# Node roots on VectorE, node rows normalised behind the coming visit's rows, three row buffers

## What is computed

```python
x = x + segment_sum(layernorm(x)[src] * edge_weight[:, None], dst) @ W.T + b
h = layernorm(x)                      # (h - mean) / sqrt(var + 1e-5)
logits = h @ gate_w + gate_b
idx = argmax(softmax(logits)); prb = softmax(logits)[idx]
# a token keeps its place if fewer than C tokens before it chose its expert
y = relu(h @ w1[idx] + b1[idx]) @ w2[idx] + b2[idx]
x = x + y * prb * kept
```

## Time and profile before

| what | value |
|---|---|
| median of 3 runs | 2467.34 us (2462.58 to 2469.74) |
| the profiled execution | 2467.59 us, span 2465.7 us, mean granted TensorE clock 0.855 |
| PE busy | 1823.3 us (74%) |
| POOL busy | 1794.0 us (73%) |
| DVE busy | 1164.4 us (47%) |
| ACT busy | 1099.5 us (45%) |

### The profile page before, as it was taken

How to read it: one execution, slowest core, us unless ns; L and a number is a source line. 1 busy time by engine, 2 the same in 40 slices (tenths; PEclk the granted TensorE clock), 3 DMA queues, 4 the chain that set the end, 5 groups by cost and what they waited for, 6 DMA issues and landing times.

```text
span 2465.7 us, 35440 instructions
## 1 busy us (share of the span) xinstructions
PE 1823.3 (74%) x9798; PEld 1185.8 (48%) x9798; DVE 1164.4 (47%) x5806; ACT 1099.5 (45%) x2565; POOL 1794.0 (73%) x1873
## 2 busy tenths in 40 slices
PE   2333466666888898777777777776887887787699
PEld 1111233333555565455444544554554555554698
DVE  7767443334454454444444444344544544444332
ACT  5667523333545454344434434343543444453343
POOL 6677777777777677777777777777777777777571
PEclk9999975555988899788888888888988988998799
DMA  6566433335553564445445454544554455556567
GB/s 225 187 210 200 121 105 113 113 112 190 155 156 114 161 214 117 152 118 188 118 116 190 116 188 118 188 117 154 155 190 154 117 191 155 190 156 189 180 237 266
DMA packets 139883, 397.04 MB, mean 161 GB/s; under 512 B 36197, under 2 KB 62821, under 8 KB 129046
## 3 DMA queue, kind: packets, MB, share of 16 engines
q0 software_dynamic: 89712, 244.29, 33.4%
q1 hardware_dynamic: 46276, 137.66, 16.2%
q10 hardware_dynamic: 3698, 12.80, 1.4%
HBM read 498.88 MB, written 42.89 MB: 220 GB/s over the span
## 4 chain that ended last, share of the span: by engine, by line
POOL 52%; issue 19%; PE 13%; DVE 8%; ACT 5%; DMA 1%; SPq 0%; DVEq 0%; POOLq 0%; ACTq 0%
POOL msg L621 49%; PE ps L980 5%; ACT msg L735 3%; POOL rows_by_expert L649 3%; DVE wsl L1136 3%; PE ps L968 2%; PE ps L879 2%; PE ps L870 1%; PE ps L959 1%; DVE wsl L1139 1%; DMA hin<-rows_by_expert 1%; DMA msg<-normed,src_sb 1%; POOL out_x L655 1%; ACT wsl L701 0%; PE ps L950 0%
## 5 line engine op out<-in xcount | busy, mean ns | idle before, releaser
L621 POOL DMA_INDIRECT msg<-normed,src_sb x1462 | 1398.1, 956 | 457.4 <-issue 445.2
L870 PE MATMUL ps<-msg,onehot 128*32 128x256 f32 x3332 | 435.2, 505 | 231.1 <-DMA msg<-normed,src_sb 206.9
L1177 DVE TENSOR_TENSOR aggT<-aggT,ps 128x192 f32 x294 | 104.7, 356 | 879.8 <-PE ps L879 856.1
L980 PE MATMUL ps<-wsl,hmid 128*128 128x256 f32 x1680 | 401.4, 394 | 1.5 <-ACT hmid L791 1.5
L744 ACT COPY pairs<-ps 128x256 f32<-128x256 f32 x294 | 111.4, 379 | 618.5 <-PE ps L870 617.6
L879 PE MATMUL ps<-shift,pairs 128*128 128x96 f32 x1176 | 237.3, 334 | 180.5 <-ACT pairs L744 180.5
L980 PEld LDWEIGHTS ps<-wsl,hmid 128*128 128x128 f32 x1680 | 322.9, 197 | 71.9 <-issue 29.5
L950 PE MATMUL ps<-wsl,hTf 128*128 128x512 f32 x680 | 350.1, 662 | 0.5 <-ACT hTf L777 0.5
L870 PEld LDWEIGHTS ps<-msg,onehot 128*32 128x32 f32 x3332 | 139.7, 128 | 413.1 <-DMA msg<-normed,src_sb 256.8
L879 PEld LDWEIGHTS ps<-shift,pairs 128*128 128x128 f32 x1176 | 191.6, 231 | 246.0 <-ACT pairs L744 242.1
L791 ACT ACTIVATE hmid<-ps,wsl 128x128 f32<-128x128 f32 x840 | 230.5, 381 | 133.3 <-PE ps L968 71.2
(11 more groups left out here) (128 smaller groups left out, 2283.3 us busy)
## 6 DMA issues: line engine op xcount, KB each, us to landing
wsl<-in_wsecond SPq DMA_DIRECT2D x105, 1152.0 KB
wsl<-in_wfirst SPq DMA_DIRECT2D x105, 1028.0 KB
msg<-normed,src_sb POOLq DMA_INDIRECT x1462
xrow<-in_x SPq DMA_DIRECT2D x97, 128.0 KB, 2.3
wsl<-in_x SPq DMA_DIRECT2D x24, 512.0 KB, 4.1
normed<-wsl ACTq DMA_DIRECT2D x24, 512.0 KB, 3.0
hin<-rows_by_expert SPq DMA_DIRECT2D x89, 130.0 KB
msg<-in_x,src_sb POOLq DMA_INDIRECT x204
```

The source lines that it names most:

```text
L621: pool.indirect_dma_start(out=msg[:, m + j, :], out_offset=None, in_=x if t < RAW else ln_dram, in_offset=bass.IndirectOffsetOnAxis(ap=src ...
L870: last = nc.tensor.matmul(ps[h * QWIN:(h + 1) * QWIN, t % 2, 0:D], onehot[:, j, :], msg[:, j, :], start=i == 0, stop=i == QUARTERS[q][h] - 1)
L980: last = nc.tensor.matmul(ps[:, Y, 0:D], hmid[:, c, :], w2_at(v % 2)[:, c, :], start=c == 0, stop=c == FC - 1)
```

## The change

The root of a node's variance is no longer ACT's. DVE computes the reciprocal root itself, in eight linked instructions: half of the variance plus epsilon; a first value from its bits, made with a negative sign; and three Newton steps of two instructions, each of which turns the sign, so that the third gives the positive result. The waits between DVE and ACT for it go. ACT's normalising of the node's tile becomes an event of its own, `nn`, which stands behind the load and the norm of the coming visit's rows and ahead of `turn`; at the end of the list it keeps its place behind `x2`. The rows of visits have three buffers instead of two, and two small tiles (`ids`, `fin`) now lie over the first 105 columns of the sources and the weights.

```diff
@@ schedule_of
         if coming is not None:
             once("hl", coming)
             once("hn", coming)
+        if stage[1] is not None:
+            events.append(("nn", stage[1]))
         events.append(("turn", t))
         events.append(("add", t))
...
-    events += [("gnn", a), ("ra", c), ("rk", c), ("x2", a), ("rb", c), ("pads",)]
+    events += [("gnn", a), ("ra", c), ("rk", c), ("x2", a), ("nn", a), ("rb", c), ("pads",)]
...
-    events += [("lg", a), ("ra", a), ("x2", b)]
+    events += [("lg", a), ("ra", a), ("x2", b), ("nn", b)]
@@ tiles and waits
+HBUFS = 3
+ROOT_BITS = float(0x5F3759DF - (1 << 22) - (1 << 31))
-        hin = sb("hin", [P, 2, ROW])
+        hin = sb("hin", [P, HBUFS, ROW])
-        ids = sb("ids", [P, V], I32)
-        fin = sb("fin", [P, V])
+        ids, fin = src_sb[:, 0:V], wgt[:, 0:V]
...
-                elif v >= 2:
-                    sp.wait_ge(s_z, v - 1)
+                elif v >= HBUFS:
+                    sp.wait_ge(s_z, v + 1 - HBUFS)
@@ scalar
-            def node_root(n):
-                act.wait_ge(s_mv, n + 1)
-                root(sd[:, :], mv[:, 1:2]).then_inc(s_sd, 1)
...
-                elif kind == "x2":
-                    node_root(key[0])
+                elif kind == "nn":
                     node_norm(key[0])
@@ vector, node(n)
-                dve.bn_aggr(mv[:, :], st6[:, :]).then_inc(s_mv, 1)
+                link(dve.bn_aggr(mv[:, :], st6[:, :]))
                 link.mark(dve.tensor_scalar(row[:, X_ID:X_ID + 1], pid, float(n * P), None, ALU.add))
-                dve.wait_ge(s_sd, n + 1)
-                link(dve.reciprocal(row[:, X_RSTD:X_RSTD + 1], sd[:, :]))
+                half, near, step = sd[:, 0:1], sd[:, 1:2], sd[:, 2:3]
+                link(dve.tensor_scalar(half, mv[:, 1:2], EPS, 0.5, ALU.add, ALU.mult))
+                link(dve.tensor_scalar(near.bitcast(I32), half.bitcast(I32), -0.5, ROOT_BITS, ALU.mult, ALU.add))
+                for to in (near, near, row[:, X_RSTD:X_RSTD + 1]):
+                    link(dve.scalar_tensor_tensor(out=step, in0=near, scalar=half, in1=near, op0=ALU.mult,
+                                                  op1=ALU.mult))
+                    link(dve.scalar_tensor_tensor(out=to, in0=step, scalar=-1.5, in1=near, op0=ALU.add,
+                                                  op1=ALU.mult))
```

More of the change, by code:

```diff
@@ L264, in gnn_moe_kernel @@
     assert max(V - NT, 0) * D + (V - FULL) * ROW <= RING * SUBS[0] * D
-    assert D == 2 * P and E8 == 8 and LAST_ROWS > 0 and NC * KD >= NT * D and V - NT <= G
+    assert V <= RAW_GROUPS * G and D == 2 * P and E8 == 8 and LAST_ROWS > 0 and NC * KD >= NT * D and V - NT <= G
     ln_dram = nc.dram_tensor("normed", (N, D), F32).ap()
@@ L287, in gnn_moe_kernel @@
         eps = sb("eps", [P, 1])
-        sd = sb("sd", [P, 1])
+        sd = sb("sd", [P, 3])
         wg_sb = sb("wg_sb", [P, KD, D])
@@ L358, in rows_at @@
             if v < FULL:
-                return hin[:, v % 2, :]
+                return hin[:, v % HBUFS, :]
             start = max(V - NT, 0) * D + (v - FULL) * ROW
@@ L363, in rows_sem @@
         def rows_sem(v):
-            return s_hin[v % 2] if v < FULL else s_last[v - FULL]
+            return s_hin[v % HBUFS] if v < FULL else s_last[v - FULL]
         def rows_used(v):
-            return 16 * (v // 2 + 1) if v < FULL else 16
+            return 16 * (v // HBUFS + 1) if v < FULL else 16
         space = wsl[:, :, :].rearrange("p a b -> p (a b)")
@@ L403, in gnn_moe_kernel @@
         s_xt = [sem(f"s_xt{u}") for u in range(XBUFS)]
-        s_n1, s_x2, s_mv, s_sd, s_stat, s_h, s_tr, s_hTs, s_log, s_ls, s_exp, s_choice, s_rank, s_route = (
-            sem(q) for q in ("s_n1", "s_x2", "s_mv", "s_sd", "s_stat", "s_h", "s_tr", "s_hTs", "s_log", "s_ls", "s_exp", "s_choice",
+        s_n1, s_x2, s_stat, s_h, s_tr, s_hTs, s_log, s_ls, s_exp, s_choice, s_rank, s_route = (
+            sem(q) for q in ("s_n1", "s_x2", "s_stat", "s_h", "s_tr", "s_hTs", "s_log", "s_ls", "s_exp", "s_choice",
                              "s_rank", "s_route"))
@@ L409, in gnn_moe_kernel @@
         s_plan = sem("s_plan")
-        s_hin = [sem(f"s_hin{b}") for b in range(2)]
+        s_hin = [sem(f"s_hin{b}") for b in range(HBUFS)]
         s_last = [sem(f"s_last{b}") for b in range(V - FULL)]
```

## The result

The changed kernel takes 2470.2 us, the kernel before 2465.1 us (medians of 15 runs each): a ratio of 1.0024, 95% interval 1.0014 to 1.0034. That is 5.1 us slower, inside the 0.3% that was called no change, where a gain to 2456.5 us was forecast, and 2 us above the stated range of 2450 to 2468 us. The profiled execution has a span of 2467.7 us against 2465.7.

What follows compares the result with a forecast made beforehand. POOL's gather issue was taken to bound the kernel, leaving only its 10.9 us wait between 600 and 900 us to gain, plus 0.2 us at the end: 2467.6 - 10.9 - 0.2 = 2456.5 us, range 2450 to 2468.

Steps and rivals of the forecast that it cites:

- What bounds the kernel: Whole loop: POOL's gather issue sets the pace; only its 10.9 us wait for PE, 600 to 900 us, can be gained.
- Roots off ACT: ACT: 98 roots and 194 table loads go, 278 us of busy time; worth nothing in the loop after 900 us.
- Eight DVE instructions: DVE's node chain: 2.12 us from moments to L1233 against 0.74, so the node comes 1.38 us later where ACT was ready.
- the norm's move: Dense stretch: copies and transposes up to 3.2 us earlier, second layer 2.0 us earlier, cycle 15.9 us instead of 17.9.
- the bound that I had named as enough: Dense stretch: any gain over 0.8 us a visit is enough to clear all 10.9 us of POOL's wait.
- a second layer at the lower clock as a rival: Dense-stretch cycle gains under 0.8 us: second layer 4.27 us instead of 3.46, 5 us come back, 2462.4 us; chance 0.08.
- the slower rival: POOL's gathers slowed by DVE's new operands, 26 us in all, so 2482.6 us; chance 0.07.
- Three buffers: Visits' row transfers: start up to 4.8 us earlier with a third buffer, costed at nothing since POOL's pace hides it.
- The end: After the last gather: node 96's DVE chain takes 2.1 us instead of 2.3, 0.2 us gained; the rest as before.
- The rival that the end gives it back: End: two short row landings become long, 9.3 us lost, so 2465.8 us, no change; chance 0.16.

Runs made afterwards that it cites:

- e1: The changed kernel with the root back on ScalarE and one reciprocal on VectorE, moved norm and three row buffers kept: 0.9967 of the kernel before, 2458.4 us.
- e12: The kernel before with only the node's norm moved behind the coming visit's rows, roots on ScalarE, two row buffers: 0.9973 of the kernel before, 2454.2 us.
- e5: The changed kernel with four unused products ahead of PE's wait for the slots, node tiles 15 to 33: 0.9967 of the kernel before, 2454.6 us.
- e11: The changed kernel with two row buffers instead of three, run where the kernel before takes 2461.2 us: 1.0027 of the kernel before.
- e9: The changed kernel with two row buffers instead of three, run where the kernel before took 2944.2 us: 0.9983 of the kernel before.

## Why the prediction was wrong

*What bounds the kernel* held. POOL's pace sets the loop, the dense stretch is the only place with something to gain, and 10.9 us is the most it gives: the five kernels with three exact steps or the root on ACT that clear the wait end 0.27 to 0.35% under the kernel before, 7 to 9 us.

*Roots off ACT* held in size (2 loads left at the two lines, 806 us of ACT's time against 820) and was worth nothing: e1 and e12 make all 194 loads and are 0.3% faster than the kernel before. What helps is not a free ACT but that the copies no longer stand behind the node's norm. That move alone was priced rightly: 15.9 us a visit were forecast, and e1 and e12 have 15.9 and 16.0.

*Eight DVE instructions* were sized well: from the moments' start to L1237 778.48 - 776.48 = 2.00 us where 2.12 were forecast, 0.20 for an operation with constants and 0.25 with a column as scalar. That is 1.26 us later than now, not 1.38. The sentence after it is wrong. It names the shift matrix and the add as what is queued behind on DVE and calls them covered. Behind them stand two one-hot operations and the slots, and for the slots PE waits.

*The step that failed* is in the norm's move: "PE's transposes and all that PE has behind them can move up by as much as 3.2 us, and ACT's order decides". PE's order from there on is transposes, the next third's sums, the node tile's transpose, the second layer. I followed the node tile to ACT's norm and did not read the third wait in `turn_node`, for the slots of the tile before. In the kernel before it was met in time, since the copies held PE back even longer, so the trace of before shows almost nothing of it: a wait that one removed wait had hidden. Counted from the moments' start, the second layer was forecast at 781.4 - 777.23 = 4.2 us and starts at 781.88 - 776.48 = 5.4: 1.2 us of the 2.0 a visit are gone and 0.8 are left, just the bound that I had named as enough. (Over all thirteen visits the cycle without its second layer falls from 17.9 - 3.9 = 14.0 to 18.1 - 5.0 = 13.1 us, 0.9 less.)

*The clock* took the remainder. I priced a second layer at the lower clock as a rival (0.08) but as a state that comes and goes, not as what follows PE's idle gap, wherever the change puts that gap. From 3.9 to 5.0 us on average is 1.1 us a visit. 17.9 - 0.8 + 1.1 = 18.2, where 18.1 was measured; and e5, which changes the clock and no wait, measures 16.5. The 0.8 is no gain of waiting alone, since the transposes and sums run at the higher clock now; how it divides was not tried.

*Port contention*, the slower rival (0.07), did not occur: the mean gather is 955 ns in the changed kernel against 956. (The sum there, 2456.5 + 26, is 2482.5 and not 2482.6.) Gathers that lie over 0.5 us or more of the one-hot operations take 1.03 us on average in the kernel before (24 of them, 600 to 900 us) and 1.01 in the changed one (27), those over none of it 0.95 in both. The Trainium skill's rule ("GPSIMD Engine Reference", section "8. Key points") agrees with that as far as the one-hot operations go, and does not show for one-column operands.

*Three buffers* at nothing: right, and e11 measures it. SP's wait for a free buffer is gone and has become the next one in its order, the second weights' wait for `z`, 406.1 us before:

```profile
SPq L574 <- DVEq L1309: 455.7, 100, 9.9
```

*The end* was to gain 0.2 us and lost 0.9. The part that was priced, node 96 from the moments to L1237, did gain: 1.99 us against 2.38. But from the last gather to the end of the span it is 2467.7 - 2261.3 = 206.4 us against 205.5, with row landings of 4.62, 2.05 and 8.37 us where the earlier trace rows has 4.28, 1.97 and 7.79. The rival that the end gives it back did not decide.

What stays open: of the 5.1 us between the medians the profiled executions show 2.4 in POOL's waits, 1.8 of it made good by gathers that are shorter in sum, and 0.9 at the end. Single executions of either kernel scatter over some 10 us, so one profile each can't place the rest. And the second layer's clock varies from visit to visit under like gaps (3.46 at 745.53, 6.11 at 762.39, each behind a gap of 3.1 us); what picks between them was not tried.

## What to carry to other kernels

When you take an instruction out of an engine's way, list every wait of the instruction that will then be next, also those the trace shows as free: they may be met in time only because of the wait that you remove. Then ask what the engine does behind the gap: if it is PE, price the work that follows at both clock levels, and look at which work that now is. And test the parts of a change one at a time; here the move alone is 0.3% faster, the arithmetic alone 0.9% slower, and together they come out 0.2% slower.

## What the runs showed of the hardware

Work that nothing needs can pay: four unused products of 0.5 us each per cycle make the changed kernel 0.6% faster (0.9967 against 1.0024 of the kernel before), as they keep TensorE's granted clock at 0.98 instead of 0.89 from 600 to 870 us. Eight keep it at 0.99 and make the kernel slower (1.0058), since they outlast the gap. It also matters where a low stretch lies: by the window's mean the changed kernel has the better clock of the two (0.89 against 0.87) and the slower second layers (5.0 against 3.9 us).

Linked DVE operations of one column start 0.18 to 0.20 us apart with constants (776.94 to 777.13 for a busy time of 0.15) and 0.25 with a column as scalar (777.13 to 777.38); unlinked neighbours of one to eight columns start 0.07 to 0.10 apart (776.69 and 776.76; 780.81 and 780.89). So here the link is about half of such an operation's price or more.

Where the kernel before takes 2944.2 us, the same kernels have another bound. It isn't that transfers take longer: the packets of POOL's queue took 28.4% of e9's span of 2927.8 us and 33.5% of e11's 2461.1, 831 and 824 us, and those of SP's queue 401 us both times. POOL's gathers, each as short as ever, wait for an event that the profile can't place and calls remote, and for PE:

```profile
L624 POOL DMA_INDIRECT msg<-normed,src_sb x1462 | 1394.6, 954 | 810.5 <-issue 396.4 <-remote 267.9 <-PE ps L868 146.2
```

In such a pause several engines stand still and go on together (e9's timeline near 1508 us):

```profile
1507.97 0.35 DVE L1175 TENSOR_TENSOR aggT<-aggT,ps 128x192 f32 x1 [8.54 <-remote]
1507.98 2.18 ACT L790 ACTIVATE hmid<-ps,wsl 128x128 f32<-128x128 f32 x8 [5.58 <-remote]
...
1508.42 1.00 POOL L624 DMA_INDIRECT msg<-normed,src_sb  x1 [2.74 <-remote]
```

What the event is stays open. There the move alone showed no gain (1.0017, 0.9997 to 1.0038), and the Newton steps with the move and two buffers no loss (0.9983). A gain of 0.3% that hangs on one stretch's pace is shown only where that pace holds.
